# Operands of the split projections read in other orders: Q and V by alternating halves, g with a step of four, K's tiles in turns of banks

## What is computed

```python
xn = layernorm(x) * scale + bias
q, k, v = xn @ Wq + bq, xn @ Wk + bk, xn @ Wv + bv      # k, v masked by token
q = softmax(q, over a head's features); k = softmax(k, over tokens)
attn = einsum('bhse,bhsd->bhed', k, v)                   # per head, a small matrix
y = einsum('bhtd,bhed->bhte', q, attn)
h = silu(layernorm(y) * (1 + film_scale) + film_shift) @ film_out_W + film_out_b
return x + h
```

## Time and profile before

| | us |
|---|---|
| median of 3 runs | 920.95 (920.02 to 922.26) |
| the profiled execution | 920.86 |
| its span, first to last instruction | 918.7 |
| PE busy | 895.4 (97%) |
| DVE busy | 598.9 (65%) |
| ACT busy | 398.6 (43%) |
| POOL busy | 283.4 (31%) |
| mean granted clock | 0.996 |

### The profile page before, as it was taken

How to read it: one execution, slowest core, us unless ns; L and a number is a source line. 1 busy time by engine, 2 the same in 40 slices (tenths; PEclk the granted TensorE clock), 3 DMA queues, 4 the chain that set the end, 5 groups by cost and what they waited for, 6 DMA issues and landing times.

```text
span 918.7 us, 16124 instructions
## 1 busy us (share of the span) xinstructions
PE 895.4 (97%) x5994; PEld 747.5 (81%) x5994; DVE 598.9 (65%) x1293; ACT 398.6 (43%) x607; POOL 283.4 (31%) x305
## 2 busy tenths in 40 slices
PE   4989999999999999999999999999999999999998
PEld 3768888888888888887788888888888888888876
DVE  5757756675676667656696666656756576576764
ACT  5326345434443534344363544335335343444433
POOL 2013423314242231424124342142422314242520
PEclk9989999999999999999999999999999999999999
DMA  6643030020302003032540401203020030301202
GB/s 213 231 181 139 2 137 0 40 97 0 137 0 103 34 0 137 0 138 56 190 187 1 149 1 47 91 0 137 0 107 30 0 137 0 137 0 49 89 1 91
DMA packets 20813, 70.94 MB, mean 77 GB/s; under 512 B 4857, under 2 KB 4905, under 8 KB 14641
## 3 DMA queue, kind: packets, MB, share of 16 engines
q1 hardware_dynamic: 20784, 70.56, 20.1%
HBM read 53.78 MB, written 16.78 MB: 77 GB/s over the span
## 4 chain that ended last, share of the span: by engine, by line
PE 95%; DVE 2%; issue 1%; ACT 0%; POOL 0%; SPq 0%; DVEq 0%; ACTq 0%
PE psum_w L395 57%; PE psum_k L395 19%; PE psum_k L620 6%; PE psum_t L610 3%; PE psum_t L445 3%; PE psum_t L458 3%; PE psum_k L585 3%; PE psum_t L422 1%; PE psum_t L431 1%; DVE x_in L686 0%; DVE y L971 0%; DVE k_max L875 0%; DVE gate L756 0%; DVE w_low_q L694 0%; DVE y_stats L978 0%
## 5 line engine op out<-in xcount | busy, mean ns | idle before, releaser
L1146 POOL TENSOR_TENSOR xT_low<-xT,xT_high 128x512 fp32r<-128x512 f32 x60 | 77.2, 1286 | 214.0 <-ACT xT_high L1040 212.5
L908 DVE TENSOR_TENSOR q<-psum_w,bias_q 128x512 f32<-128x512 f32 x64 | 44.2, 691 | 98.4 <-PE psum_w L395 98.4
L395 PE MATMUL psum_k<-w_high_k,xT_high 128*128 128x512 f32 x256 | 104.7, 409 | 0.5 <-DVE y L971 0.5
L395 PE MATMUL psum_w<-w_high_v,xT_high 128*128 128x512 f32 x256 | 101.3, 396 | 0.2 <-DVE emb_cols L881 0.2
L1063 ACT ACTIVATE gate<-psum_t,film_shift,film_scale 128x512 f32<-128x512 f32 x60 | 46.6, 776 | 126.5 <-PE psum_t L458 95.9
L395 PE MATMUL psum_k<-w_high_k,xT_low 128*128 128x512 f32 x256 | 100.3, 392 | 0.0
L395 PE MATMUL psum_w<-w_high_q,xT_high 128*128 128x512 f32 x256 | 100.1, 391 | 0.0
L395 PE MATMUL psum_k<-w_low_k,xT_high 128*128 128x512 f32 x256 | 100.0, 391 | 0.0
L395 PE MATMUL psum_w<-w_low_v,xT_high 128*128 128x512 f32 x256 | 99.7, 389 | 0.0
L395 PE MATMUL psum_w<-w_high_v,xT_low 128*128 128x512 f32 x256 | 99.7, 389 | 0.0
L395 PE MATMUL psum_w<-w_high_q,xT_low 128*128 128x512 f32 x256 | 99.6, 389 | 0.0
(11 more groups left out here) (129 smaller groups left out, 1835.5 us busy)
## 6 DMA issues: line engine op xcount, KB each, us to landing
x_in<-x_between_layers SPq DMA_DIRECT2D x9, 1024.0 KB, 4.8
x_res<-in_x SPq DMA_DIRECT2D x8, 1024.0 KB, 6.7
x_between_layers<-x_res SPq DMA_DIRECT2D x8, 1024.0 KB, 3.8
x_in<-in_x SPq DMA_DIRECT2D x7, 1024.0 KB, 4.8
x_res<-x_between_layers SPq DMA_DIRECT2D x7, 1024.0 KB, 6.8
out_x<-x_res SPq DMA_DIRECT2D x7, 1024.0 KB, 3.8
raw_weights<-in_L_cond_film_emb_W SPq DMA_DIRECT2D x4, 1024.0 KB, 5.9
raw_weights<-in_L_cond_W_emb SPq DMA_DIRECT2D x4, 1024.0 KB, 5.2
```

Source lines behind the costliest of these rows:

```text
L395: mm = pe.matmul(bank, lhs[:, c, rows_of_tile], rhs[w][:, c, :], start=(c == 0 and n == 0), stop=(c == CHUNKS - 1 and n == 2))
L908: dve.tensor_tensor(q[:, t, :], psum_w[:, t % 2, :], bias_q[:, :], ALU.add)\
L1146: pool.tensor_tensor(xT_low[:, c, :], xT[:, c % 2, :], xT_high[:, c, :], ALU.subtract)\
```

## The change

Four operands are laid out or read in another order; each output is unchanged, since writer and reader are changed together.

- Q: w_high_q and w_low_q are stored with the even columns of a row in its first half and the odd ones in its second. `columns` gives the view in the old order: two columns from two halves, then the next two. ACT's cast and DVE's subtraction write through the same view.
- V: the same with runs of 16 columns (64 bytes) from either half.
- g: gT_high and gT_low hold token s of tile t at s*4+t instead of t*128+s, so that a tile is read as the stationary operand with a step of four elements (16 bytes), and written so by ACT and DVE.
- K, all iterations but the first: tiles in two pairs. In a pair, each of the three products of a chunk is issued for one tile and then for the other, whose accumulators are in different banks. Tile 0 waited for xT_low alone and the rest found it there; now the pair does. The transposes of y stand in the middle of the second pair.

```diff
+LINE = 16
+        def columns(w, m):
+            if m == Q:
+                return w.rearrange("p (a b) -> p b a", a=2)
+            if m == V:
+                return w.rearrange("p (a b r) -> p b a r", a=2, r=LINE)
+            return w
+        def raw_columns(w, m):
+            if m == Q:
+                return w.rearrange("p (b a) -> p b a", a=2)
+            if m == V:
+                return w.rearrange("p (b a r) -> p b a r", a=2, r=LINE)
+            return w
+        def tokens(g):
+            return g.rearrange("p (s t) -> p t s", t=TILES)
+        def by_tile(g):
+            return g.rearrange("p (t s) -> p t s", t=TILES)
...
-                            mm = pe.matmul(bank, lhs[:, c, rows_of_tile], rhs[w][:, c, :],
+                            x_tile = tokens(lhs[:, c, :])[:, t, :] if spread else lhs[:, c, rows_of_tile]
+                            mm = pe.matmul(bank, x_tile, columns(rhs[w][:, c, :], w),
...
+            def alternating_products(tiles, before):
+                for c in range(CHUNKS):
+                    before(c)
+                    for n, (x, w) in enumerate(((xT_high, w_high), (xT_high, w_low), (xT_low, w_high))):
+                        for t in tiles:
+                            mm = pe.matmul(psum_k[:, t, :], x[:, c, of_tile(t)], w[K][:, c, :],
+                                           start=(c == 0 and n == 0), stop=(c == CHUNKS - 1 and n == 2))
+                            if c == CHUNKS - 1 and n == 2:
+                                mm.then_inc(k_psum, 1)
...
-                split_products([(t, psum_w[:, t % 2, :]) for t in tiles], *gated_of(j), O, o_psum,
-                               gate_split if 0 in tiles else None)
+                split_products([(t, psum_w[:, t % 2, :]) for t in tiles], gT_high, gT_low, O, o_psum,
+                               gate_split if 0 in tiles else None, spread=True)
...
-                    for t in range(TILES):
-                        if t == 0:
-                            pe.wait_ge(y_ready, TILES * (i - 1) + 3)
-                        if t == 2:
-                            pe.wait_ge(y_ready, TILES * i)
-                        if with_output and t == 3:
+                    def y_turned(c):
+                        if with_output and c == CHUNKS // 2:
                             turn_y(i - 1, 0)
                             turn_y(i - 1, 1)
-                        project([(t, psum_k[:, t, :])], K, k_psum, k_ready if t == 0 else None)
+                    pe.wait_ge(y_ready, TILES * (i - 1) + 3)
+                    alternating_products((0, 1), k_ready)
+                    pe.wait_ge(y_ready, TILES * i)
+                    alternating_products((2, 3), y_turned)
...
-                dve.tensor_tensor(w_low[m][:, c, :], raw[:, slot * CHUNKS + c, :], w_high[m][:, c, :], ALU.subtract)\
+                dve.tensor_tensor(columns(w_low[m][:, c, :], m), raw_columns(raw[:, slot * CHUNKS + c, :], m),
+                                  columns(w_high[m][:, c, :], m), ALU.subtract)\
...
-                dve.tensor_tensor(low[:, c, :], gate[:, c % 2, :], high[:, c, :], ALU.subtract)\
+                dve.tensor_tensor(tokens(gT_low[:, c, :]), by_tile(gate[:, c % 2, :]), tokens(gT_high[:, c, :]),
+                                  ALU.subtract)\
...
-                    act.copy(w_high[m][:, c, :], raw[:, at % 2 * CHUNKS + c, :]).then_inc(w_high_ready, 1)
+                    act.copy(columns(w_high[m][:, c, :], m), raw_columns(raw[:, at % 2 * CHUNKS + c, :], m))\
...
-                act.copy(gated_of(j)[0][:, c, :], gate[:, c % 2, :]).then_inc(g_high_ready, 1)
+                act.copy(tokens(gT_high[:, c, :]), by_tile(gate[:, c % 2, :])).then_inc(g_high_ready, 1)
```

More of the change, by code:

```diff
@@ L385, in _, with split_products @@
         def _(pe):
-            def split_products(tiles, high, low, w, done, before=None):
+            def split_products(tiles, high, low, w, done, before=None, spread=False):
                 for c in range(CHUNKS):
@@ L827, in split_gate @@
                 dve.wait_ge(g_high_ready, CHUNKS * j + c + 1)
-                high, low = gated_of(j)
-                dve.tensor_tensor(low[:, c, :], gate[:, c % 2, :], high[:, c, :], ALU.subtract)\
+                dve.tensor_tensor(tokens(gT_low[:, c, :]), by_tile(gate[:, c % 2, :]), tokens(gT_high[:, c, :]),
+                                  ALU.subtract)\
                    .then_inc(g_low_ready, 1)
@@ L1027, in split_weights @@
                 for c in range(CHUNKS):
-                    act.copy(w_high[m][:, c, :], raw[:, at % 2 * CHUNKS + c, :]).then_inc(w_high_ready, 1)
+                    act.copy(columns(w_high[m][:, c, :], m), raw_columns(raw[:, at % 2 * CHUNKS + c, :], m))\
+                       .then_inc(w_high_ready, 1)
             def scale_x(i, layer):
```

## The result

The changed kernel takes **946.47 us** (median of four runs, 946.23 to 947.48), the kernel before 920.94: a ratio of 1.0281 with a 95% interval of 1.0266 to 1.0296, so it is slower by 25.5 us. The forecast was 1082 us. The direction was right and the time lies in the range of 918 to 1110, but the move is a sixth of the one forecast. The term that was to make it gives time back instead, so that the right direction is luck: the loss comes from terms that were put near 0.

What follows compares the result with a forecast made beforehand. PE was taken to bound the kernel (busy 97%, 95% of the chain), through the pitch of its 3072 split products. 920.9 + 160 (Q) + 0 (V) + 0 (g) - 3 + 1 + 3 (waits) = 1082 us, range 918 to 1110.

Steps and rivals of the forecast that it cites:

- Q, +160 us: Q's 768 products: columns from alternating halves slow each to 435 ns, 208 ns more, +160 us.
- I take the upper end: Q's pitch: of the bounds, the pace of fp32 columns, 435 ns per product, was chosen over no cost.
- one DVE pair: Two DVE tensor_tensor of 32 elements, 195 ns contiguous and 216 ns with step four, taken as evidence that each jump costs.
- V, 0: V's 768 products in runs of 16 columns: taken as 0, between bounds of +10 and -10 us.
- g, 0: O's 720 stationary loads of g with a step of four: taken as 0, upper bound +77 us.
- K's banks, 0: K's 48 products in turns of banks: no gain expected, at most -10 us.
- the wait for xT_low, -3: K's start: chunk-by-chunk waits for POOL's xT_low disappear in 14 iterations, -3 us.
- The chain to V's tile 2, +1 (0 to 5): DVE and ACT between K's end and V's tile 2: PE stalls 0 to 0.4 us in 14 iterations, +1 us.
- The first iteration of layer 1, +3 (1.9 to 4.2): Q's weight split on DVE delays the last maximum after K, so PE waits once before V's tile 2, +3 us.
- Rival 3: 13.5 ns of every pitch is a cost of in-order or one-bank reading; alternating hides it, 891 or 901 us; chance 0.07.
- the regular 32 cycles: Argument for the in-order reading cost: 226.8 ns is 32 cycles above 512, one per 16 columns, too regular for a wait.
- rival 1: Jumps are free for PE and only the waits move, 919 to 927 us; chance 0.20.

Runs made afterwards that it cites:

- e6: Against the kernel before, weights read with constant steps: K 2 columns, V 4, Q 8, O 16; g and K's tiles as before; 1582.86 us.
- e10: Against the kernel before, weights read with steps of K 32, V 64, Q 128 columns, O in twos at distance 128; 1309.47 us.
- e2: Only V's part of the change (runs of 16 columns from alternating halves) against the kernel before; 931.49 us, ratio 1.0117.
- e11: K's tile pairs and g's step of four together, V and Q as in the kernel before; 945.42 us, ratio 1.0286.
- e3: Only g's part of the change (written and read with a step of four) against the kernel before; 934.43 us, ratio 1.0148.
- e4: Only K's part of the change (products in pairs of tiles) against the kernel before; 920.34 us, ratio 0.9991.
- e7: Against the kernel before, all four weights read by alternating halves column by column, g and K's tiles unchanged; 894.83 us, ratio 0.9710.
- e12: Against the kernel before, all four weights by alternating halves, K in pairs, DVE's split of Q's weights moved, g unchanged; 891.04 us, ratio 0.9678.
- e8: Against the kernel before, weights stored as before, Q and V read and write results in runs of two and four from alternating halves; 1016.07 us.

## Why the prediction was right or wrong

- **Q, +160 us: wrong.** The step that failed is "I take the upper end". It took the pace of fp32 rows as the price of a jump, supported by one DVE pair. Q's pitch is 215.8 ns, and its products give back 8.4 us. The row on DVE was a row on reading and writing with a step, and DVE and ACT do pay for that (0.41 and 0.50 us per 512 columns where they write so). It says nothing on PE's moving rows in two streams. The upper end itself was no invention: constant steps stand at 431 to 487 ns (e6, e10). What was missed is that two streams by turns are not a step.
- **V, 0: the term is mis-sized.** It stood at 13 ns by the price of Q's jumps, and was set to 0 as nearest to the unchanged row. The pitch is 240 ns, 13.3 more, +10.2 us (e2: +10.3). That the old price hits it is chance: by that price, Q should have paid too.
- **g, 0: wrong by half a mechanism.** The upper bound had the load at 295 ns; it is 310. But it had the 107 ns paid on each product, and the pitch grew by 6 ns only; with the 122 ns on the first product of each of 49 stretches that is +10.2 us. The room of 39 ns under the pitch was not the limit: loads of 310 ns run at a pitch of 235. Why the mean pitch grows at all no run shows.
- **K's banks, 0 and the wait for xT_low, -3: right.** The pitch is 227 within pairs, the wait is gone, and K gives back 2.5 us.
- **The chain to V's tile 2, +1 (0 to 5): the mechanism was right and the size wrong.** Three of its numbers were short. The order costs 0.72 us, not 0.52: DVE stands idle for 0.20 us between the two maxima. The strided writes cost 1.13 us, not 1.0, and the room is 1.08 us, not 1.13. So PE stalls 0.77 us where the forecast's worst case had 0.4, and the first product after a wait costs 0.11 more. Without V's part (e11) that is 13.0 us outside the first iteration of layer 1; in the change, where V's slower products give 0.32 us of room back, it is 8.2. e3, e4 and e11 show that both parts are needed for it.
- **The first iteration of layer 1, +3 (1.9 to 4.2): the wait was right, the total is 5.6.** The interval before V's tile 2 grew by 4.0 us, at the upper end; 1.5 us more are the products at half the granted clock behind it, which the forecast didn't have. PE's V product there starts at 494.76.

```profile
494.76 0.64 PE L420 MATMUL psum_w<-w_high_v,xT_high 128*128 128x512 f32 x1 [3.82 <-ACT v L1131]
```

- **Rival 3** (13.5 ns of each pitch is a cost of reading one row in order, and alternating hides it, 0.07) is what happened to Q, and neither V nor K's banks followed. Its argument from the regular 32 cycles was the better reading of the earlier trace rows. The argument against it, that the pitch is the same in K, O, V and Q, was a little off: V and Q stand at 226.7 ns and K and O at 229. Had Q been given it, with the upper bounds for V and the waits, the sum would have been 920.9 - 8.4 + 10 - 3 + 5 + 4 = 929 without g and 939 with a g of 10.
- The range held the time because it had to reach from the forecast to rival 1, not because its terms bounded it: errors of 10 (V), 10 (g) and 7 us (the chain) lay inside a gap of 160.

## What to carry to other kernels

Read a pitch that lies above the engine's plain column time as room that may be won, and try the order of the moving columns: here two streams read by turns took 2.9% off a kernel that is bound by PE (e7), and 3.2% with two smaller moves (e12). A price taken from another engine's row is a bound and should not be the forecast, above all where it makes up the whole sum. Changes that each use up a part of one queue's slack must be added on that queue before they are priced, since each alone can look free and the two together are paid in every iteration.

## What the hardware showed that I had not expected

- Moving columns of fp32r in order take 226.7 to 229 ns for 512, and 215.8 ns when they come from two places at least 16 bytes apart by turns. Runs of two between the same places take 334 ns, constant steps 431 to 487.
- A stationary tile read with a step of 16 bytes loads in 310 ns instead of 188, and nearly all of it stays hidden (mean pitch 229 to 235).
- A result of a matmul written in runs of two or four columns, 1 KB apart, costs nothing that shows (e8).
- In the changed kernel the granted clock fell to half just after PE had resumed from a wait of 3.8 us, and V's products stood at 427 ns instead of 240 until it was back.
- ACT and DVE pay 0.50 and 0.41 us per 512 columns for writes that go to another 16 bytes with each column (0.62 to 1.12 us, 0.68 to 1.09). ACT pays nothing for turns inside 16 bytes or for runs of 16 (V's casts stay at 614 ns).
